# Gated cross-attention and quantised feed-forward on one core: two low halves taken in PSUM, a weight rounding on GpSimd, a semaphore that counts by one

## The reference

```python
def fixed_quant(x, width, frac_width):
    scale = jnp.float32(2.0 ** frac_width)
    return jnp.clip(jnp.round(x * scale), imin, imax) / scale
...
x = x + jnp.tanh(g_xattn[0]) * _L0_xattn_ref(_layernorm(x, axis=-1), ctx_1024, Wq, Wk, Wv, Wo, bo)
x = x + jnp.tanh(g_ffn[0]) * _L0_ffn_ref(_layernorm(x, axis=-1), w1, b1, w2, b2)
...
attn = jax.nn.softmax(jnp.einsum('bhnd,bhmd->bhnm', q, k) * scale, axis=-1)
out = jnp.einsum('bhnm,bhmd->bhnd', attn, v)
...
xq, wq, bq = fixed_quant(x, 8, 4), fixed_quant(w, 8, 6), fixed_quant(b, 8, 6)
h = relu(fixed_quant(xq @ wq1.T + bq1, 8, 4)); out = fixed_quant(h, 8, 4) @ wq2.T + bq2
```

## Time and profile before

| | us |
|---|---|
| median of 3 runs | 119.93 (119.35 to 120.69) |
| the profiled execution's own time | 119.76 |
| its span in the profile | 117.9 |
| TensorE busy, share of the span | 113.5, 96% |
| VectorE busy | 97.7, 83% |
| GpSimd busy | 86.9, 74% |
| ScalarE busy | 77.1, 65% |

### The profile page before, as it was taken

How to read it: one execution, slowest core, us unless ns; L and a number is a source line. 1 busy time by engine, 2 the same in 40 slices (tenths; PEclk the granted TensorE clock), 3 DMA queues, 4 the chain that set the end, 5 groups by cost and what they waited for, 6 DMA issues and landing times.

```text
span 117.9 us, 2921 instructions
## 1 busy us (share of the span) xinstructions
PE 113.5 (96%) x1017; PEld 103.6 (88%) x1017; DVE 97.7 (83%) x224; ACT 77.1 (65%) x172; POOL 86.9 (74%) x160
## 2 busy tenths in 40 slices
PE   7999999999999999989999999999999999999990
PEld 2599979999799999979999999999999999897870
DVE  3039889998999999989999999999797979648981
ACT  4138679887779795996757575758483739548420
POOL 5003739877585859898999988995999999988720
PEclk9999999999999999999999999999999999999999
DMA  3998699400000000000020002000200020020204
GB/s 87 360 357 257 218 362 393 193 21 3 3 0 6 0 0 3 0 6 0 0 89 0 6 0 89 3 6 0 89 0 0 8 89 0 0 89 6 88 12 167
DMA packets 5711, 8.86 MB, mean 75 GB/s; under 512 B 1191, under 2 KB 2242, under 8 KB 5698
## 3 DMA queue, kind: packets, MB, share of 16 engines
q1 hardware_dynamic: 5466, 8.34, 20.1%
q10 hardware_dynamic: 232, 0.34, 0.8%
HBM read 6.59 MB, written 2.10 MB: 74 GB/s over the span
## 4 chain that ended last, share of the span: by engine, by line
POOL 29%; DVE 22%; PE 22%; issue 5%; DVEq 0%; POOLq 0%
POOL hid L372 7%; POOL probs L310 6%; PE sc_ps L913 6%; POOL x_sb L393 5%; PE of_ps L950 4%; DVE probs L649 4%; PE h_ps L981 4%; POOL yq L326 4%; POOL rstd L320 3%; DVE mx L641 3%; PE of_ps L996 3%; DVE den L661 3%; DVE pT L690 2%; DVE st L700 2%; DVE x_sb L695 2%
## 5 line engine op out<-in xcount | busy, mean ns | idle before, releaser
L913 PE MATMUL sc_ps<-a_sb,xT 128*128 128x308 f32 x192 | 31.4, 312 | 0.0
L950 PE MATMUL of_ps<-u_sb,pT 128*128 128x256 f32 x240 | 31.0, 281 | 0.0
L950 PEld LDWEIGHTS of_ps<-u_sb,pT 128*128 128x128 f32 x240 | 29.6, 188 | 0.3 <-issue 0.2
L913 PEld LDWEIGHTS sc_ps<-a_sb,xT 128*128 128x128 f32 x192 | 27.6, 188 | 0.8 <-ACT xT L436 0.4
L499 ACT ACTIVATE hid_q<-h_ps,b1z 128x256 int8<-128x256 f32 x58 | 24.5, 494 | 3.6 <-PE h_ps L981 3.6
L453 ACT ACTIVATE probs<-probs,rstd 128x616 f32<-128x616 f32 x16 | 13.1, 816 | 21.0 <-DVE probs L649 20.9
L310 POOL TENSOR_TENSOR probs<-probs,rden 128x616 f32<-128x616 f32 x16 | 19.5, 1220 | 5.8 <-DVE rden L664 5.8
L372 POOL CAST hid<-hid_q 128x512 bf16<-128x512 int8 x27 | 15.8, 610 | 2.0 <-ACT hid_q L499 2.0
L981 PE MATMUL h_ps<-x2T,w1T 128*128 128x256 bf16 x128 | 16.8, 274 | 0.0
L641 DVE TENSOR_REDUCE mx<-sc_ps 128x8 f32<-128x616 f32 (+1 forms) x18 | 13.0, 722 | 2.8 <-PE sc_ps L913 1.9
L649 DVE TENSOR_TENSOR probs<-sc_ps,mx 128x616 f32<-128x616 f32 (+1 forms) x18 | 13.1, 729 | 1.4
(11 more groups left out here) (137 smaller groups left out, 177.3 us busy)
## 6 DMA issues: line engine op xcount, KB each, us to landing
w_sb<-in_L_ffn_w_dram SPq DMA_DIRECT2D x2, 1024.0 KB, 12.3
out_dram<-x_sb SPq DMA_DIRECT2D x7, 256.0 KB, 2.0
x_sb<-in_x_dram SPq DMA_DIRECT2D x4, 256.0 KB, 6.8
x_sb<-in_x_dram SPq DMA_DIRECT2D x1, 1024.0 KB, 12.4
wq_sb<-in_L_xattn_Wq_dram SPq DMA_DIRECT2D x1, 512.0 KB, 4.9
wv_sb<-in_L_xattn_Wv_dram SPq DMA_DIRECT2D x1, 512.0 KB, 6.5
wo_sb<-in_L_xattn_Wo_dram SPq DMA_DIRECT2D x1, 512.0 KB, 8.5
wk_sb<-in_L_xattn_Wk_dram SPq DMA_DIRECT2D x1, 256.0 KB, 3.0
```

The source lines that it names most:

```text
L913: ins = nc.tensor.matmul(sc_ps[:, a, 0:HALF], xT[:, T % 2, p, c, :], a_sb[:, q, T // TB, c, HALF * a:HALF * a + HALF], start=first, stop=last)
L950: ins = nc.tensor.matmul(attn_ps, pT[:, T % 2, p, P * c:P * c + P], u_sb[:, q, MC * (T // TB) + c, :], start=first, stop=last)
```

## The change

The low probabilities of tiles 3 and 4 are no longer subtracted by VectorE. After `scores(s+2)` in steps 3 and 4 TensorE multiplies minus the identity with the high part (one matmul of 512 columns, one of 128) and adds it to `pT_ps`; ScalarE copies the low part out, in step 3 between the second and the third `u_low_copy`, in step 4 between the two `hidden_round` calls. For these tiles the five transposes of `probsT` clear a bank's state only at the first chunk of each bank. The second half of w2 is rounded by GpSimd at the end of its `rstd_first` in step 3, no longer by ScalarE. The maximum adds one to `max_ready` for every instruction.

```diff
+LOW_FROM_PSUM = (3, 4)
+POOL_HALVES = (1,)
...
+        pT_rest = sem("pT_rest")
...
+            def round_w2(h):
+
+                if h == POOL_HALVES[0]:
+                    pool.wait_ge(w2_in, 16)
+                src, dst = w2_sb[:, :, :].rearrange("p a b -> p (a b)"), w2q[:, :, :].rearrange("p a b -> p (a b)")
+                nc.gpsimd.tensor_scalar(dst[:, 1024 * h:1024 * h + 1024], src[:, 1024 * h:1024 * h + 1024], WQ, 1.0, ALU.mult,
+                                        ALU.mult).then_inc(w2_rounded, 1)
...
                 if s == 2:
                     output_bias()
+                if s == 3:
+                    round_w2(1)
...
+            def pT_low_copy(T):
+
+                act.wait_ge(pT_rest, 1 + LOW_FROM_PSUM.index(T))
+                nc.scalar.copy(pT[:, T % 2, 1, :], pT_ps).then_inc(pT_low, 1)
...
                 if s >= 6:
                     rowsT_second(s - 2)
+                if s >= 4 and s in LOW_FROM_PSUM:
+                    pT_low_copy(s)
                 if s >= 4:
                     hidden_round(s - 4, 1)
...
                 if s == 3:
-                    for n in range(3):
+                    for n in range(2):
                         u_low_copy(n)
-                    round_weights(w2_in, w2_sb, w2q, w2_rounded, (1,))
+                    pT_low_copy(3)
+                    u_low_copy(2)
...
                 nc.vector.tensor_reduce(mx[:, i, h].rearrange("p (a h) -> p a h", a=len(banks)),
-                                        sc_v[:, banks[0]:banks[-1] + 1, :, :], AX.X, ALU.max).then_inc(max_ready, len(banks))
+                                        sc_v[:, banks[0]:banks[-1] + 1, :, :], AX.X, ALU.max).then_inc(max_ready, 1)
...
-                dve.wait_ge(max_ready, 2 * T + banks[-1] + 1)
+                dve.wait_ge(max_ready, 2 * T + banks[-1] + 1 if T < 2 else T + 3)
...
-                    probsT_low(s)
+                    if s not in LOW_FROM_PSUM:
+                        probsT_low(s)
...
+                rest = T in LOW_FROM_PSUM
                 for c in range(MC):
-                    ins = nc.tensor.transpose(pT_ps[:, P * c:P * c + P].bitcast(F32R), probs_words[:, T % 2, P * c:P * c + P],
-                                              ident_r[:, :])
+
+                    ins = nc.tensor.matmul(pT_ps[:, P * c:P * c + P].bitcast(F32R), probs_words[:, T % 2, P * c:P * c + P],
+                                           ident_r[:, :], start=not rest or c in (0, 4), stop=not rest or c in (3, 4),
+                                           is_transpose=True, skip_group_check=rest)
...
+            def probsT_rest(T):
+
+                pe.wait_ge(consts, 4)
+                pe.wait_ge(pT_high, T + 1)
+                pe.wait_ge(xT_ready, T + 4)
+                for first, end in ((0, 512), (512, HMP)):
+                    ins = nc.tensor.matmul(pT_ps[:, first:end], minus_ident[:, :], pT[:, T % 2, 0, first:end], start=False,
+                                           stop=True, skip_group_check=True)
+                ins.then_inc(pT_rest, 1)
...
                 if live(s + 2):
                     scores(s + 2)
+                if s in LOW_FROM_PSUM:
+                    probsT_rest(s)
```

## The result

The changed kernel takes 119.0 us against 119.9 before (medians of 20 runs each); the ratio is 0.992, 95% interval 0.990 to 0.995. The forecast was no change. The profiled execution took 118.8 us with a span of 117.0.

What follows compares the result with a forecast made beforehand. GpSimd was taken to decide when `ffn_out(0)`'s second half starts. GpSimd +0.02, TensorE 0, signal 0 and the rest unchanged gave 119.8 us profiled, 119.9 as a median; range 119.0 to 120.7.

Steps and rivals of the forecast that it cites:

- The bound: At the second half of `ffn_out(0)`, 52.57 us: VectorE's gain counts only if GpSimd gets there earlier.
- the chain on GpSimd before 42.4: Sign that the forecast is right: the chain of waits is already on GpSimd before softmax(5) starts at 42.4 us.
- VectorE's part: Steps 3 and 4: two removed subtractions relieve VectorE by 2 x 0.70 = 1.40 us, but `residual(3)` then waits for `attend(3)`.
- TensorE's part: Steps 3 and 4: added matmuls cost 0.74 us, a copy wait 0.1, within 0.87 of slack; `ffn_out(0)` reached at 52.53.
- GpSimd's part: Step 3: rounding w2 takes 1.07 us, fills the 0.97 gap before softmax(5), which starts 0.02 us later.
- The maximum's signal: Gap from VectorE's maximum to the subtraction: counting by one could gain 0.25 us, but a second wait stays; taken as nothing.
- half-way case: Partial form of the faster rival: rounding at its lower bound plus the signal's 0.25 us gives 119.4; chance 0.14.
- Unchanged after 52.57: From the second half of `ffn_out(0)` to the span's end: 117.9 - 52.57 = 65.3 us, as before.
- Rival (a): Steps 3 and 4: VectorE's relief goes through to the end, -1.40 us, 118.5; chance 0.06 in full.
- (b): Step 3: a dearer GpSimd rounding makes the kernel slower, 120.5 or 121.4 us; chance 0.13.
- (c): TensorE late at `ffn_out(0)`, by added matmuls at their upper bound or a longer copy wait: 120.2 us; chance 0.15.

Runs made afterwards that it cites:

- e2: Changed kernel with the signal counted by two and w2's second half rounded by ScalarE, both as before, leaving only the low probabilities from PSUM: ratio to before 0.998.
- e4: Changed kernel with only the maximum's signal counted by two as before: ratio to before 0.997.
- e7: Changed kernel with the second half of w2 rounded by ScalarE again, signal still counted by one: ratio to before 0.995.
- e11: Changed kernel with w2's second half rounded by ScalarE and one more never-waiting wait on GpSimd before the output bias rounding: ratio to before 0.995.
- e3: Kernel before with only the second half of w2 rounded by GpSimd in step 3: ratio to before 0.999.
- e13: Kernel before with one more never-waiting wait on VectorE before tile 5's statistics, first loop; profiled only: 14.30 us from first maximum to that of tile 3.
- e8: Kernel before with two more never-waiting waits on VectorE at tile 5's statistics in step 0, signal still by two: ratio to before 0.999.
- e9: Kernel before with one more never-waiting wait on GpSimd in step 2, before the output bias rounding: ratio to before 0.997.
- e5: Changed kernel measured again without any edit: ratio to before 0.994.
- e12: Changed kernel measured a third time without any edit: ratio to before 0.993.
- e1: Kernel before with only the maximum's signal counted by one: ratio to before 0.9985.
- e6: Changed kernel with one more never-waiting wait on VectorE in step 0, before tile 5's statistics: ratio to before 0.995.

## Why the prediction was wrong

- **The bound.** Right: GpSimd and TensorE arrive together at the second half of `ffn_out(0)`, and an edit in steps 3 and 4 counts by what GpSimd does. e2 shows the low halves at 0.05 us earlier there and 0.00 at VectorE's last result; e4, with the rounding too, is 0.1 later there and 0.03 at the last result. The sign "the chain on GpSimd before 42.4" did not come, since TensorE's lead was spent: where GpSimd has no rounding (e7, e11), TensorE's loads wait for nothing.
- **VectorE's part.** Right: two slots of 0.70 gained, idle behind `attend(3)` instead (0.55 us).
- **TensorE's part.** Right in size: 0.36 for a rest (0.37 taken), 0.12 of waiting for the copy (0.1). TensorE reached `ffn_out(0)` 0.43 us later in e4 (39.07 - 0.18 = 38.89) and 0.46 later in e2 (38.92) than before (38.97 - 0.51 = 38.46), where I had 0.48. That its loads still waited 0.17 us, and not under 0.1, comes mostly from GpSimd, which was 0.1 later than I had it.
- **GpSimd's part.** The rounding took 1.04 us (1.07), but it started 0.08 after the reported end of line 309 (40.76 against 40.68), not 0.04 before. So softmax(5) was 0.10 us later in e3, counted from the first maximum, where I had 0.02. A later GpSimd by 0.1 is a loss of 0.1 at `ffn_out(0)`: 39.07 against 38.97.
- **The maximum's signal.** This is the step that failed, by a mechanism that I didn't have: the term stands in the sum at 0, and with the signal's edit 0.3 to 0.4 us went. I weighed the 0.05 us between maximum and subtraction and took nothing; that gap is still there after the change (28.48 is 0.09 behind 28.39). What went was 0.3 us of idle time ahead of the maximum of tile 3, marked as issue in the view that I read. I had the row before me and didn't ask what it was, so I had no rival for it. The half-way case's 0.25 for the signal was the price of another mechanism. e13 and e8 show that it isn't the counting: one or two waits more, ahead of it, do it too. Of 0.40 at the maximum of tile 3, 0.1 is given back at the rounding, and 0.33 is left at `ffn_out(0)` (38.97 - 38.64), and in this profile it goes through to the end: 101.34 to 101.03 us from the first maximum to VectorE's last result. In the other two profiles of the changed kernel that is 101.17 and 101.18, so 0.2 to 0.3 are left.
- **"Unchanged after 52.57", 65.3 us.** The second term that failed. It was 117.0 - 51.96 = 65.04. The last 0.3 are GpSimd's end, changed by one instruction more on that engine. The forecast took what lies behind the last result as fixed, and e9 shows that it isn't.
- **The size in whole runs.** By the traces 0.3 and 0.3 make 0.6 us, 0.995; by e5 and e12 it is 0.5, 0.996. The three measurements of the changed kernel say 0.992, 0.994 and 0.993; two of the three intervals hold both. Whether 0.2 to 0.4 us more lie in the opening, whose length varies by 1.9 us among the profiles, was not settled.

Rival (a), VectorE's relief passing through, had no part in it, though the time came out on its side; (b) and (c) did not happen.

## What to carry to other kernels

Before a small gain is put down to an edit, lay a few waits that never wait into the old kernel, on the engines whose streams the edit alters: here three of them gain as much as the change, within the noise of the runs. Read the idle rows marked as issue on the bounding engine as carefully as the waits, since they have a price (0.3 us here, 0.25% of the kernel) that an unrelated edit can add or remove. Relief of an engine counts only after the next two engines have been followed to the place where they meet.

## What the runs showed that was not expected

- An idle time of 0.3 us on VectorE with no wait, and 0.47 in e1 between maximum and subtraction, each followed 0.6 to 0.8 us after its end by an 8 KB transfer on the instruction queue. A change of one instruction in VectorE's stream ahead of it makes it vanish or move. That a fetch causes it fits all profiles but is not shown: the trace doesn't name the engine that a transfer serves, and the rule for where it falls was not found: the fixed count that I expected failed in e6 and e13.
- The end of the kernel, after VectorE's last result has started, takes 2.65 or 2.95 us by one instruction on GpSimd, in 11 and seven profiles.
- A GpSimd tensor_scalar from f32 to int8 runs at (1.04 - 0.19) / 1023 = 0.83 ns a column at 1024 columns, near the 0.86 at 256.
